# Hyena block with a gated feed-forward on one core: the sums of every half's last output block move from GpSimd to VectorE, and the temporaries are split two and two

## The reference

```python
u  = x @ in_proj_w.T + in_proj_b                 # 512 -> 1536
uc = short causal convolution of u, 3 taps, per channel, + short_b
x0, x1, v = split(uc)
k  = filter network over positions (512 x 512, depends on the weights alone)
y  = (causal_conv(v * x1, k) + filter_bias * (v * x1)) * x0     # long convolution, by FFT
x  = layernorm(x + y @ out_proj_w.T + out_proj_b)               # LN1
gate, up = x @ Wg.T, x @ Wu.T                    # 512 -> 1408, 8-bit codes with a scale
x  = layernorm(x + (silu(gate) * up) @ Wd.T)                    # LN2
```

## Time and profile before

| | |
|---|---|
| median of 3 runs | 1119.78 us (1116.08 to 1120.39) |
| the profiled execution | 1114.26 us, span of its instructions 1112.5 us |
| busy: PE, DVE, ACT, POOL | 93%, 70%, 42%, 58% of the span |
| granted clock of PE, mean | 0.975 of full speed |
| one round of the steady part (469.31 to 530.91 us) | 61.60 us |

### The profile page before, as it was taken

How to read it: one execution, slowest core, us unless ns; L and a number is a source line. 1 busy time by engine, 2 the same in 40 slices (tenths; PEclk the granted TensorE clock), 3 DMA queues, 4 the chain that set the end, 5 groups by cost and what they waited for, 6 DMA issues and landing times.

```text
span 1112.5 us, 18049 instructions
## 1 busy us (share of the span) xinstructions
PE 1035.8 (93%) x6378; PEld 838.2 (75%) x6378; DVE 780.6 (70%) x1437; ACT 467.6 (42%) x995; POOL 650.7 (58%) x695
## 2 busy tenths in 40 slices
PE   4966879999999999999999999999999999979996
PEld 2545758887888888788888888888888888857774
DVE  4456667687777778787777878787777778775443
ACT  3454544443434444443435344443444444423242
POOL 1367576567575667566574666576574766675211
PEclk9988889999999999999999999999999999989998
DMA  4254521222223211322122212312121212213332
GB/s 152 91 183 133 169 77 30 73 81 76 58 76 96 80 55 47 101 62 86 49 84 87 86 49 67 104 50 84 50 76 49 85 58 64 70 50 94 105 90 81
DMA packets 52215, 90.58 MB, mean 81 GB/s; under 512 B 6362, under 2 KB 11098, under 8 KB 52126
## 3 DMA queue, kind: packets, MB, share of 16 engines
q1 hardware_dynamic: 51362, 89.16, 26.5%
q10 hardware_dynamic: 764, 0.27, 0.1%
HBM read 78.14 MB, written 11.27 MB: 80 GB/s over the span
## 4 chain that ended last, share of the span: by engine, by line
PE 75%; DVE 9%; POOL 6%; ACT 4%; issue 4%; DMA 2%; ACTq 0%; POOLq 0%; DVEq 0%; SPq 0%
PE gate_up L907 11%; PE gate_up L908 11%; PE bank L780 10%; PE bank L782 9%; PE bank L781 9%; PE down L918 6%; PE down L919 6%; PE bank L870 3%; PE bank L892 2%; POOL acc L578 1%; PE spectrum L780 1%; PE spectrum L782 1%; PE spectrum L781 1%; DVE xT_lo L662 1%; PE bank L871 1%
## 5 line engine op out<-in xcount | busy, mean ns | idle before, releaser
L549 ACT ACTIVATE hid<-gate_up,gate_scale 128x256 f32<-128x256 f32 x176 | 83.3, 473 | 240.7 <-PE gate_up L908 239.4
L698 DVE TENSOR_TENSOR tmp<-spectrum,filt 128x512 f32<-128x512 f32 x256 | 172.8, 679 | 0.0
L780 PE MATMUL bank<-xT_hi,win_hi 128*128 128x512 f32 x384 | 162.2, 422 | 6.8 <-DVE cx L674 3.0
L584 POOL TENSOR_TENSOR acc<-acc,tmp 128x256 f32<-128x256 f32 x160 | 123.9, 775 | 74.0 <-DVE tmp L698 62.8
L907 PE MATMUL gate_up<-x2T_hi,wg_sb 128*128 128x256 f16 x704 | 165.3, 275 | 0.0
L908 PE MATMUL gate_up<-x2T_lo,wg_sb 128*128 128x256 f16 x704 | 163.3, 273 | 0.0
L908 PE MATMUL gate_up<-x2T_lo,wu_sb 128*128 128x256 f16 x704 | 163.3, 273 | 0.0
L907 PE MATMUL gate_up<-x2T_hi,wu_sb 128*128 128x256 f16 x704 | 163.3, 273 | 0.0
L782 PE MATMUL bank<-xT_hi,win_lo 128*128 128x512 f32 x384 | 154.5, 402 | 0.0
L918 PE MATMUL down<-wd_sb,hid_hi 128*128 128x512 f32 x352 | 148.7, 423 | 6.1 <-DVE tmp L727 4.6
L781 PE MATMUL bank<-xT_lo,win_hi 128*128 128x512 f32 x384 | 154.2, 402 | 0.0
(11 more groups left out here) (121 smaller groups left out, 2206.5 us busy)
## 6 DMA issues: line engine op xcount, KB each, us to landing
wd_sb<-wd_scratch SPq DMA_DIRECT2D x176, 256.0 KB, 2.6
xstage<-in_x SPq DMA_DIRECT2D x32, 256.0 KB, 3.9
x<-in_x SPq DMA_DIRECT2D x32, 256.0 KB, 2.8
out<-x SPq DMA_DIRECT2D x32, 256.0 KB, 3.2
x<-in_win SPq DMA_DIRECT2D x12, 256.0 KB, 2.9
x<-in_wd SPq DMA_DIRECT2D x5, 256.0 KB, 3.0
wd_scratch<-x SPq DMA_DIRECT2D x5, 256.0 KB, 2.8
acc<-in_decay SPq DMA_DIRECT2D x4, 256.0 KB
```

The source lines that it names most:

```text
L584: G.tensor_tensor(acc[:, i, 0, :], acc[:, i, 0, :], t[:, 1, :], ALU.subtract)
L698: TT(dst, spectrum[j % 2][:, :, :], k_part, ALU.mult).then_inc(made_done, 1)
L780: mm(out_ap, ah, bh, start=k == 0, stop=False)
```

## The change

The part-1 sums and the part-0 sums with j > 0 of output block i = 3 leave POOL: `acc` returns at once for them, and DVE adds directly behind each such product (new lines 712 to 720 of the changed kernel). Of the four temporaries, two (2 and 3) now belong to these products (`own`, counted in `own_added`), and two (0 and 1) to all others (`temp`, counted in `temp_added`). Per half these are seven products: three of part 0 and four of part 1.

```diff
-        temp = {s: k for k, s in enumerate(s for s in steps if s[0] == "ln2" or s[0] == "mul" and (s[2] or s[4]))}
+        own = count([s for s in steps if s[0] == "mul" and s[3] == TB - 1 and (s[2] or s[4])], "mul")
+        temp = {s: k for k, s in enumerate(s for s in steps if s[0] == "ln2" or s[0] == "mul" and (s[2] or s[4])
+                                           and s not in own)}
...
         def temp_of(step):
-            return tmp[:, temp[step] % 4, :, :]
+            return tmp[:, 2 + own[step] % 2, :, :] if step in own else tmp[:, temp[step] % 2, :, :]
...
                 elif kind == "psplit":
-                    act.wait_ge(temp_added, temp["mul", n, i, i, 1] + 1)
+                    last = ("mul", n, i, i, 1)
+                    if last in own:
+                        act.wait_ge(own_added, own[last] + 1)
+                    else:
+                        act.wait_ge(temp_added, temp[last] + 1)
...
                 elif kind == "acc":
                     first, second = ("mul", n, j, i, 0), ("mul", n, j, i, 1)
+                    if second in own:
+                        continue
...
                     step = ("mul", *at)
-                    if step not in temp:
+                    if step in own:
+                        if own[step] >= 2:
+                            dve.wait_ge(own_added, own[step] - 1)
+                        dst = temp_of(step)
+                    elif step not in temp:
...
                     else:
-                        if temp[step] >= 4:
-                            dve.wait_ge(temp_added, temp[step] - 3)
+                        if temp[step] >= 2:
+                            dve.wait_ge(temp_added, temp[step] - 1)
                         dst = temp_of(step)
...
                     TT(dst, spectrum[j % 2][:, :, :], k_part, ALU.mult).then_inc(made_done, 1)
+                    if step in own:
+                        dve.wait_ge(made_done, made[step] + 1)
+                        if own[step]:
+                            dve.wait_ge(own_added, own[step])
+                        if part == 0:
+                            TT(acc[:, i, :, :], acc[:, i, :, :], dst, ALU.add).then_inc(own_added, 1)
+                        else:
+                            TT(acc[:, i, 0, :], acc[:, i, 0, :], dst[:, 1, :], ALU.subtract)
+                            TT(acc[:, i, 1, :], acc[:, i, 1, :], dst[:, 0, :], ALU.add).then_inc(own_added, 1)
...
                 elif kind == "ln2":
-                    dve.wait_ge(temp_added, temp[step] - 3)
+                    dve.wait_ge(temp_added, temp[step] - 1)
```

More of the change, by code:

```diff
@@ L263, in build @@
         bank_read, made_done = sem("bank_read"), sem("made_done")
-        temp_added = sem("temp_added")
+        temp_added, own_added = sem("temp_added"), sem("own_added")
         x_hi_done = sem("x_hi_done")
```

## The result

| | before | after |
|---|---|---|
| median, same chip | 1117.93 us (1114.08 to 1120.39, 4 runs) | 1188.6 us (1185.03 to 1190.88, 4 runs) |
| the profiled execution | 1114.26 us, span 1112.5 | 1185.03 us, span 1183.2 |
| granted clock of PE, mean | 0.975 | 0.974 |

The ratio is 1.0643 (95% interval 1.0617 to 1.0669): the kernel is slower by 6.4%. The forecast was 1170 us, 1140 to 1192.

A forecast was written before the change was run, and what follows sets the result against it. PE bounds the kernel, busy 61.14 of 61.60 us in a steady round. 12 x (1.7 + 2.6) = 51.6, plus 2.6 and 2.5, less 1.6, gave +55 on 1114.26: 1169, named 1170 us, range 1140 to 1192.

The forecast's parts named there:

- No slack at `op` of beat 6 and at `dn` of beat 10, PE not to be made faster in the middle: Both start 0.06 us behind DVE's work, so DVE's lateness shows there; a change can only remove end gaps or make new.
- The price of a sum, 0.72 and 0.80: On DVE a part 0 adds 0.72 us, a part 1 0.80; 0.84 is the upper bound for the wide sum.
- Beat 2 costs nothing: Beat 2: one part 1 of 0.80 us is covered by DVE's idle 1.71 us before the conv of beat 3.
- The ring, 1.05 and 1.7, of which 0.9 reaches beat 5: Beat 3: with two places the second `ln2` product starts 1.05 us later, the next 1.7; 0.9 carries into beat 5.
- Beat 5, 1.1 or 2.3, middle 1.7: Shift ends 1.1 us later if DVE gets in before POOL, 2.3 if POOL does; `op` is later by the same.
- Beats 7 to 9, 2.0 to 3.1, middle 2.6: Sums make `hmul` and `hid_lo` of beat 9, and PE with them, 2.0 to 3.1 us late, middle 2.6.
- Rounds 1, 2 and 16, together +2.5: Sums partly fill PE's gaps, partly lengthen the LN1 chain: +2.5 us together, of which round 16 takes 1.5.
- POOL's relief, -1.6: Steady rounds: the inverse of block 2 waits less behind POOL's sums of block 3, giving back 1.6 of 17.9 us.
- What the profile was to show: DVE x1613, 870 to 900 us busy; POOL about 491; PE waiting for DVE before `op` 1.1 to 2.3; steady round 66 us.
- That the relief decides: Rival: DVE's idle time absorbs the sums and PE gets back waits for `acc_lo`; 1100 to 1108 us, chance 0.05.
- That the ring does not count: Rival: beat 3's late products are made up before the shift, only the sums count; +30, 1144 us, chance 0.14.
- that the lateness feeds on itself: Rival: POOL's low parts of `acc` also come late and `iv` stops PE; +80, to 1200 us and above, chance 0.08.

The follow-up runs named there:

- the late sums alone: Kernel before with only block 3's sums of beats 7 and 8 (j of 2 or 3) moved to DVE, one ring of four: 1154.7 us, ratio 1.0334.
- sums_one_later: ring4_all with each moved sum one DVE instruction later, behind `hmul` or `hid_lo` instead of directly behind its product: 1163.88 us, ratio 1.0426.
- ring2_pool: Kernel before with two temporaries instead of four for all products, every sum still on POOL: 1128.62 us, ratio 1.0100.
- ring4_all: Changed kernel with all products sharing one ring of four temporaries again, sums of block 3 still on DVE: 1176.01 us, ratio 1.0528.
- sums_no_port: ring4_all with the moved sums reading the spectrum in PSUM in place of `acc`, so only one operand is in SBUF: 1155.87 us, ratio 1.0346.
- the early sums alone: Kernel before with only block 3's sums of beats 2 and 5 (j of 0 or 1) moved to DVE, one ring of four: 1138.32 us, ratio 1.0196.
- dve_sums_last_half: Kernel before with all sums of half 15 (round 16), all four blocks, on DVE and none other, ring of four: 1120.43 us, ratio 1.0041.
- the first four experiments: ring4_all, ring2_pool, the late sums alone and the early sums alone, run on one chip: 1176.01, 1128.62, 1154.7 and 1138.32 us.
- the last four: On another chip: sums_no_port, sums_one_later, dve_sums_last_half, and the latter with blocks 0 to 2 of half 0 added: 1155.87, 1163.88, 1120.43, 1118.48 us.

## Why the prediction was right

It was right in direction, mechanism and place, and short in size: 1169 against 1185.03 on the profiled execution, and 1170 against a median of 1188.6, near the upper end of its range. Point by point, by its own steps:

- **No slack at `op` of beat 6 and at `dn` of beat 10, PE not to be made faster in the middle.** It holds. All four new waits of a round are for DVE, and the late sums alone lengthen B by 2.7 us a round.
- **The price of a sum, 0.72 and 0.80.** In beat 7 the product starts at 552.63, the sum at 553.35, `hmul` at 553.96: 1.33 in place of 0.60, so 0.73. The pair of the same beat takes 0.80 (554.35 to 555.75, less 0.60). The 0.12 in it was tested by sums_one_later. The upper bound of 0.84 for the wide sum was not needed: alone it takes 0.69.
- **Beat 2 costs nothing.** It holds. The pair fits into DVE's idle time before the conv of beat 3, which is 0.92 now and was 1.71, and that conv starts as long after the start of the round as before (18.30 and 18.31 us):

```profile
519.85 0.75 DVE L680 SCALAR_TENSOR_TENSOR cx<-bank,taps,cx 128x511 f32<-128x511 f32 x1 [0.92 <-ACT cx L500]
```

- **The ring, 1.05 and 1.7, of which 0.9 reaches beat 5.** Measured 1.10 and 1.73, of which 0.86 reaches beat 5. One link was missing: I had the lateness travel on DVE to beat 5, but PE already stops in beat 3, when `dn` waits 0.84 for the same `ln2` product. With the sums on top this changes no size, since `op` of beat 6 starts right behind the conv on DVE wherever PE stopped before: 0.86 a round. It does show in the waits: `op` waits for 1.0 us and not for the 1.1 to 2.3 that I had named, the rest of the 2.15 having been lost in beat 3. Alone, in ring2_pool, the ring costs 1.0 a round, and all of it by the link that I had not seen.
- **Beat 5, 1.1 or 2.3, middle 1.7.** Measured 2.15: POOL gets the port first, in every one of the twelve rounds. In ring4_all it splits up: the two sums 1.52 and the port 1.09 (by sums_no_port), less the 1.09 that the shift no longer waits (1.24 to 0.15) and the 0.21 that `hid_lo` of beat 5 no longer does (0.63 to 0.42 in every steady round), is 1.31, and 1.29 was measured; the ring adds 0.86. The middle was mis-sized by 0.45, 5.4 us in twelve rounds; the end in which POOL gets in first, 2.3, was the one that held. I had treated the port as a race that either side may win, and it is none: the same order came out in all twelve rounds. Between two ends that a fixed schedule decides, a middle is right for no round.
- **Beats 7 to 9, 2.0 to 3.1, middle 2.6.** Measured 2.66, and here the middle was met partly by luck. The race at the port was lost in every steady round too. `hid_lo` of beat 7 in round 8, before and after:

```profile
519.85 0.74 DVE L770 TENSOR_TENSOR hid_lo<-hid,hid_hi 128x256 fp32r<-128x256 f32 x1
```

```profile
555.75 1.49 DVE L792 TENSOR_TENSOR hid_lo<-hid,hid_hi 128x256 fp32r<-128x256 f32 x1
```

  In round 8 that is the "some 0.8" of the upper end, 3.1. Two things that the forecast did not have pulled the other way: before the change `hid_lo` of beat 7 took 0.74 to 0.75 in seven of the twelve rounds and 1.00 to 1.44 in the others, and `var_eps` of beat 8 takes 0.17 now in each round, where it took 0.45, a wait for POOL that is gone. Against that, the idle time before `hmul` of beat 8, read as 0.74 in round 8, was 0.11 to 0.48 in five of the twelve.
- **Rounds 1, 2 and 16, together +2.5.** This is the term that was furthest off. Rounds 1 and 2 took 8.1 us more, where 1.0 was left for them; the rounds from 16 on took 0.1 more, not 1.5; round 3 took 3.2, not 2.6. I had said that PE has gaps there which the sums partly fill. But these gaps are waits for DVE and ACT in a row, so a later DVE lengthens them. In round 1 the two sums of beat 5 stand ahead of the conv that `ip` waits for:

```profile
94.20 0.68 DVE L711 TENSOR_TENSOR tmp<-spectrum,filt 128x512 f32<-128x512 f32 x1
94.92 1.08 DVE L717 TENSOR_TENSOR acc<-acc,tmp 128x512 f32<-128x512 f32 x1
95.92 0.68 DVE L711 TENSOR_TENSOR tmp<-spectrum,filt 128x512 f32<-128x512 f32 x1
96.63 0.79 DVE L719 TENSOR_TENSOR acc<-acc,tmp 128x256 f32<-128x256 f32 x1
...
97.68 0.73 DVE L680 SCALAR_TENSOR_TENSOR cx<-bank,taps,cx 128x511 f32<-128x511 f32 x1
```

  From the first product to the conv it is 3.48 us; before the change it was 1.34 (91.36 to 92.70). With the early sums alone rounds 1 to 3 take 7.6 us more than before, with the late ones alone 3.7. How the rest of it divides between the LN1 chain and `ip` in round 2 I did not take apart. The granted clock has a part that stays open. In these rounds it reads 0.50 of full speed in some stretches and 1.00 in the others, and where the lower ones fall differs from kernel to kernel: PE ran at 0.50 for 40.7 us of rounds 1 to 3 before the change, for 46.6 after it and for 58.0 in ring4_all, whose rounds 1 to 3 are 1.7 us longer than the changed kernel's. PE was busy for 130.65 us of these rounds against 127.98 before, so by my estimate the clock accounts for at most 2.7 of the 11.4. In round 16 the forecast had a loss of 1.5 and no gain; there the waits for `acc_lo` fell from 8.2 to 6.1 us and that for `ln2` grew from 1.1 to 3.1, and the two cancel.
- **POOL's relief, -1.6.** There was nothing to relieve in the steady rounds: of the 17.9 us in the earlier trace rows only 0.5 lie there. I had taken a total of the whole run for a property of the middle.
- **The sum.** Steady rounds 57.7 instead of 50.0 with the relief, rounds 1 and 2 8.1 instead of 1.0, round 3 0.6 more, the end 1.4 less, and 1.6 before round 1 that no term could have, since nearly all of it is the first load's: 15.6 of the 15.8 us by which 70.8 exceeds 55.
- **What the profile was to show.** DVE x1613 was right, but it is busy for 853.0 us and not 870 to 900, in part because `hid_lo` meets POOL less (mean 591 ns instead of 635) and the shift of LN2 not at all in the steady rounds. POOL is busy for 500.9 us, not 491. The steady round is 66.42 to 67.55, not 66.
- **The rivals.** That the relief decides is out: A and B both grew. That the ring does not count is out by ring2_pool. That the lateness feeds on itself is out too: the waits for `acc_lo` fell from 17.9 us to 9.0, and the parts add up. Its +80 would have come nearer to the time than the forecast, by the wrong mechanism.

The 70.7 us of the medians part like this: ring 12.6 (1188.6 to 1176.01), port of the new sums 20.1 (1176.01 to 1155.87), and 38 to 39 (to the 1117.93 and 1116.74 of the kernel before) for the time of the sums on DVE, the shift's saved wait already deducted. The runs were on different chips (ring4_all and sums_no_port), and each difference is good to a few us. The last part still has some port in it, since `hid_lo` of beat 7 takes 1.30 in sums_no_port and took 0.95 in the mean before. Of it the waits on their own product are about 9 (12 rounds x 6 x 0.12, and those of the other rounds not counted).

## What to carry to other kernels

When one engine is busy for 99% of a round, the busy share of the others says nothing on what they can take over. Look for the places where the bound engine starts right behind them, and price each instruction that you put ahead of such a place at its pitch; here that gave 4.3 us a round, and 4.8 were measured. Read a list of waits by stage before counting on it: nearly all of the waits that the change could have removed lay in the first and last rounds, where the engine that was to take the work was itself on the path. And a buffer split in two rings is a smaller ring for each: with two places the `ln2` products and the sums behind them cost 12 us, with four nothing (three were not tried). Last, where two engines hold each other up, as POOL's product does DVE's sum here (1.74 us in place of 0.69), and the order of their instructions is fixed, work out who comes first: here the order was the same in all twelve rounds, and a middle between winning and losing fits no round.

## What the runs showed of the hardware that was not expected

- A DVE sum of 128 x 512 from two operands in SBUF takes 0.69 us when POOL is quiet (the sum at 553.35), the same as with one operand in PSUM (0.691 mean in sums_no_port), and the 128 x 256 sum 0.42 (the second of the pair in beat 7 of round 8), against means of 0.424 and 0.413 with one in PSUM. So the second operand in SBUF cost nothing by itself here. It cost where POOL had started first: up to 1.09 us (1.78 for 0.69, in dve_sums_last_half).
- That cost is hidden in the means. The groups of new sums show 48 x 0.309 = 14.8 us for the wide one; 20 us came back when it was taken away. Of the difference the small sums have 2 to 3 us (437 and 443 ns in the changed kernel against 424 and 413), and `hid_lo` of beat 7, an old instruction, 2.3.
- A wait of PE costs 0.16 us more than its idle time. This is an estimate from the overlap of the matmuls' records (0.24 apart, 0.40 long); with 48 waits it is 7.7 us, and with it the waits come to 56.1 of the 57.7 us of the steady rounds. In ring2_pool it closes too: 12.1 against 12.0.
- Round 0 took 42.4 to 42.6 us in the profiled executions of the kernel before, of the changed one and of the first four experiments, and 45.5 to 45.7 in those of the last four, on another chip, ahead of any sum. The granted clock goes with it: in the last four it is 0.50 for 6.8 us from about 35 us on (by my estimate half of that, 3.4 us, is the most that it can cost), and the mean of the round is 0.91 to 0.93. In the others there is no such stretch there, and the mean is 0.99 to 1.00. PE is then busy for 40.2 instead of 37.3 us (sums_no_port, kernel before) with the same 119 matmuls. Why the clock fell there the runs do not show; the comparisons above leave it out where they go by stretches.
